# A hand-written statement order ahead of the main loop, replaced on four engines

## The chip, the cores and the metric

One core of one Trainium2 chip runs the whole program. The metric is device microseconds of that core, the median of three runs.

## What is computed

A block of 2048 tokens of width 512 goes through three layers, each with a residual: half a router layer, an attention layer, half a router layer. Cut to what matters here:

```python
def ffn(h):                         # router layer, on layernorm(x)
    logits = h @ router_weight.T + router_bias        # 64 experts
    w = top8(softmax(logits))
    return h * w.sum() + w_dense @ expert_bias
x = x + 0.5 * ffn(layernorm(x))
x = x + attention(layernorm(x))     # 8 groups of 4 heads, chunks of 128 tokens,
                                    # decay from cumulated g = softplus(x @ Win.T + dt_bias) * A
x = x + 0.5 * ffn(layernorm(x))
```

## The kernel before, in words

The tokens are 4 blocks (f = 0 to 3) of 4 chunks (i = 0 to 3) of 128. The attention runs as a long loop of 8 groups times 16 steps, one chunk a step, and its code in `step` is the same in both kernels. Ahead of the first step, every engine has its own straight list of calls; that list is written out by hand, one for TensorE (from line 999), ScalarE (from 1251), GpSimd (from 1498) and VectorE (from 1747). Engines wait for each other only through semaphores, and each engine works strictly down its list. What these lists do for each block:

- `pe_turn` (L530) transposes a chunk of x, `act_turned` (L540) copies it out as FXT, `pe_logits` (L557) multiplies it with the router weights. `dve_stats(dve, 0, ...)` (L463, L468) and `pool_rstd` (L478 to L483) make the layernorm's scale.
- `dve_logits` (L568 to L576), `dve_choose` (L582, L585), `act_exp` (L611) and `dve_weigh` (L592 to L604) pick eight experts. `pe_weights` (L621) and `act_weights` (L626) transpose the weights as FWT; `pe_mix` (L649, L650) multiplies them with the expert biases. The mix of block 0 also waits for `lows_ready`, which GpSimd raises after two operations, FEBL and WINL (L1508).
- `pool_scales` and `pool_residual` (L674) scale x, `dve_mixed` (L705) adds the mix.
- `dve_stats(dve, 1, ...)`, `act_normalise` (L715, tile XN), `pe_turn2` (L724), `act_turned2` (L730, XTH) and `dve_turned2` (L737, XTL) make the attention's input.
- `pe_dt` (L349 to L351 on WINH, WINL), `dve_dt_in`, `dve_dt_abs`, `dve_series` (L783 to L805, on 256 columns: blocks 0 and 1 as q = 0, blocks 2 and 3 as q = 1) make g. The last operation of `dve_series(dve, 0, 3)` writes NG (L805). `pe_sums`, `act_sums`, `pe_rows`, `act_rows` turn it, the SP queue sends it to memory and reads it back broadcast (ROWS), and GpSimd masks it (`mask_rows`, L1462).
- `fill(0, 0, k)` for k = 0 to 9 are the first block's projections: K, four Q, V, four gates. `swap`, `times_sin`, `times_cos`, `add_sin` rotate K and Q; `gate` (L1194) and `silu2` (L1661) finish the gates; `decay` (L1207), `decayed` (L1676), `p_hi` (L1213) and `p_lo` (L1484) build the attention weights of a chunk, `weighted_v` (L1472) and `wv_lo` (L1480) the weighted values.

The first projection inside step 0, called fill A below, goes into a bank that `silu2(0, 0, 3, 9)` must have read; `bank_free` has that wait. `decay(0, 1)` on ScalarE waits for `p_lo(0, 0)`, since both use the tile PF.

Of the kernel before, what the change touches and what calls it, by code (L numbers as in the profile page):

```python
# [19 lines left out]
ALU = mybir.AluOpType  # L20
ACT = mybir.ActivationFunctionType
# [15 lines left out]
FAR = 1.0e30  # L37
# [87 lines left out]
def build(nc, x, cos, sin, masks, wall, rwt, rb, eb2, wint, dtb, alog, gn, out):  # L125
    rows_dram = nc.dram_tensor("rows_dram", (NCH, KVH, GW), F32).ap()
    with ExitStack() as ctx:
# [46 lines left out]
        AFTER = sb("AFTER", [P, P])  # L174
# [669 lines left out]
        def _(pe):  # L844
# [158 lines left out]
            pe_turn(pe, 0, (0, 1))  # L1003
# [17 lines left out]
            pe_weights(pe, 1)  # L1021
            pe_turn2(pe, 0, (0,))
            pe_mix(pe, 1, (0, 1))
            pe_turn2(pe, 0, (1,))
            pe_mix(pe, 1, (2,))
            pe_turn2(pe, 0, (2,))
            pe_mix(pe, 1, (3,))
            pe_turn2(pe, 0, (3,))
            pe_logits(pe, 2, (2, 1, 0))
            pe_turn(pe, 3, (0,))  # L1030
            pe_logits(pe, 2, (3,))
            pe_turn(pe, 3, (1,))
# [114 lines left out]
        def _(act):  # L1147
# [833 lines left out]
```

## Time and profile before

| what | value |
|---|---|
| median of 3 runs | 1702.77 us (1702.34 to 1702.81) |
| profiled execution, its time | 1706.06 us |
| its span | 1704.2 us |
| mean granted TensorE clock | 0.989 |
| TensorE matmul busy | 97% of the span |
| VectorE, GpSimd, ScalarE busy | 83%, 72%, 66% |

The profiled execution took 3.3 us more than the median of the runs; 1.9 us of its time lies outside the span. Busy shares are means over the whole program: the stretch that the change touches is the first 105 us.

### The profile page before, as it was taken

Reading aid. Unit: us, or ns where it says so; the run is one execution under the profiler, and the core shown is the slowest. Engines: PE = TensorE matmul, PEld = TensorE weight load, DVE = VectorE, ACT = ScalarE, POOL = GpSimd, SP = SyncE. Lnnn points to the kernel's source line nnn. Section 1 sums busy time; section 2 is a strip of 40 time slices with the busy share of each in tenths; the row PEclk is TensorE's granted clock in tenths of the full one; section 3 lists DMA queues with packets and bytes.
Section 4 is the critical chain, followed back from the end, with each engine's and each line's share of the span. In section 5 each row is a group of like instructions: output and inputs, shape, how many; then the busy total and the mean of one; then the engine's idle time right before and its main releaser. Section 6 shows DMA issues by size and latency. Waiting matters only on the chain.

```text
span 1704.2 us, 34810 instructions
## 1 busy us (share of the span) xinstructions
PE 1650.2 (97%) x11470; PEld 954.6 (56%) x11668; DVE 1410.6 (83%) x3089; ACT 1119.9 (66%) x3019; POOL 1231.9 (72%) x1204
## 2 busy tenths in 40 slices
PE   7898999999999999999999999999999999999987
PEld 5554555555555555555555555555555555555554
DVE  6988788787878888787888888788888888788887
ACT  4775676766666667666766667666766666666653
POOL 4676677777777777776868768676777777777755
PEclk8999999999999999999999999999999999999998
DMA  5111011010111012010111011110110102110002
GB/s 209 32 35 52 21 45 63 32 39 20 57 50 51 20 32 75 19 51 26 57 51 44 20 38 57 38 50 20 44 63 32 38 20 64 45 37 20 26 13 100
DMA packets 39059, 76.91 MB, mean 45 GB/s; under 512 B 4832, under 2 KB 5856, under 8 KB 37856
## 3 DMA queue, kind: packets, MB, share of 16 engines
q1 hardware_dynamic: 38880, 74.66, 13.8%
q8 instruction: 95, 1.56, 0.4%
q14 instruction: 84, 0.69, 0.1%
HBM read 70.19 MB, written 4.46 MB: 44 GB/s over the span
## 4 chain that ended last, share of the span: by engine, by line
PE 76%; POOL 8%; DVE 7%; issue 5%; ACT 3%; DMA 1%; SPq 0%; DVEq 0%; POOLq 0%; ACTq 0%
PE B L350 24%; PE B L351 23%; PE B L349 22%; PE B L962 3%; POOL QS L1449 1%; PE B L557 1%; POOL WVF L1472 1%; POOL ROWS L1462 1%; POOL PL L1484 1%; PE B L909 1%; POOL RR L1491 1%; POOL WL L1442 1%; ACT QS L1170 1%; POOL KL L1456 1%; DVE ST L1706 1%
## 5 line engine op out<-in xcount | busy, mean ns | idle before, releaser
L1484 POOL TENSOR_TENSOR PL<-PF,PH 128x512 bf16<-128x512 f32 x128 | 158.2, 1236 | 300.0 <-ACT PH L1213 300.0
L351 PE MATMUL B<-WH,XTL 128*128 128x128 bf16 (+1 forms) x992 | 269.3, 296 | 1.6
L1213 ACT ACTIVATE PH<-PF 128x512 bf16<-128x512 f32 x128 | 80.7, 630 | 278.7 <-DVE PF L1676 278.7
L350 PE MATMUL B<-WL,XTH 128*128 128x128 bf16 (+1 forms) x961 | 257.6, 294 | 1.7
L349 PE MATMUL B<-WH,XTH 128*128 128x128 bf16 (+1 forms) x960 | 257.2, 294 | 0.6 <-DVE QF L1641 0.6
L350 PE MATMUL B<-XTL,WH 128*128 128x512 bf16 x640 | 243.3, 380 | 1.7
L1449 POOL TENSOR_TENSOR QS<-QS,SIN 128x512 f32<-128x512 f32 x160 | 204.6, 1279 | 47.0 <-ACT QS L1170 47.0
L349 PE MATMUL B<-XTH,WH 128*128 128x512 bf16 x609 | 231.5, 380 | 3.2 <-DVE G L1661 1.0
L351 PE MATMUL B<-XTH,WL 128*128 128x512 bf16 x610 | 231.8, 380 | 0.0
L1725 DVE SCALAR_TENSOR_TENSOR YF<-B,RR,G 128x128 f32<-128x128 f32 x512 | 143.9, 343 | 72.4 <-POOL RR L1491 72.4
L1207 ACT ACTIVATE PF<-ROWS,NG 128x128 f32<-128x128 f32 x512 | 162.8, 391 | 47.1 <-POOL ROWS L1462 46.8
L350 PE MATMUL B<-WL,ZTH 128*128 128x512 bf16 x480 | 181.9, 379 | 0.1
L351 PE MATMUL B<-WH,ZTL 128*128 128x512 bf16 x479 | 181.5, 379 | 0.0
L349 PE MATMUL B<-WH,ZTH 128*128 128x512 bf16 x478 | 181.2, 379 | 0.1
L1676 DVE SCALAR_TENSOR_TENSOR PF<-B,DT,PF 128x128 f32<-128x128 f32 x512 | 143.3, 340 | 42.9 <-PE B L351 39.3
L1685 DVE TENSOR_TENSOR YF<-B,EG 128x512 f32<-128x512 f32 x120 | 82.7, 689 | 103.8 <-PE B L962 103.8
L1462 POOL TENSOR_TENSOR ROWS<-ROWS,AFTER 128x512 f32<-128x512 f32 x128 | 162.7, 1272 | 2.7 <-DMA ROWS<-rows_dram 2.7
L1491 POOL TENSOR_TENSOR RR<-RM,HALF 128x4 f32<-128x4 f32 x128 | 144.3, 1128 | 10.1 <-POOL RM L1488 0.2
L1236 ACT ACTIVATE YF<-B 128x128 f32<-128x128 f32 x512 | 133.6, 275 | 11.8 <-DVE B L1692 10.7
L1480 POOL TENSOR_TENSOR WVL<-WVF,WVH 128x512 bf16<-128x512 f32 x120 | 139.0, 1159 | 0.0
L1472 POOL TENSOR_TENSOR WVF<-VF,WJ 128x512 f32<-128x512 f32 x120 | 138.3, 1152 | 0.1
L1646 DVE TENSOR_TENSOR QF<-QF,QS 128x512 f32<-128x512 f32 x128 | 131.3, 1027 | 6.9 <-POOL QS L1449 5.4
(213 smaller groups left out, 4474.2 us busy)
## 6 DMA issues: line engine op xcount, KB each, us to landing
ROWS<-rows_dram SPq DMA_DIRECT2D x128, 256.0 KB, 3.3
STAGE<-in_wall SPq DMA_DIRECT2D x108, 256.0 KB, 2.8
ACC<-in_x SPq DMA_DIRECT2D x3, 1024.0 KB, 9.9
out<-ACC SPq DMA_DIRECT2D x3, 1024.0 KB, 3.9
ACC<-in_x SPq DMA_DIRECT2D x4, 256.0 KB, 3.9
COS<-in_cos SPq DMA_DIRECT2D x1, 1024.0 KB, 12.2
SIN<-in_sin SPq DMA_DIRECT2D x1, 1024.0 KB, 14.5
out<-ACC SPq DMA_DIRECT2D x4, 256.0 KB, 4.3
```

The source lines that it names most:

```text
L349: nc.tensor.matmul(out_, ah, bh, start=first, stop=False)
L350: nc.tensor.matmul(out_, ah, bl, start=False, stop=False)
L351: return nc.tensor.matmul(out_, al, bh, start=False, stop=last)
L1207: ins = nc.scalar.activation(PF[:, c], ROWS[:, n % 2, c], ACT.Exp, bias=tab(NG, g, n)[:, h:h + 1], scale=-1.0)
L1449: nc.gpsimd.tensor_tensor(QS[:, sl, :], QS[:, sl, :], SIN[:, t0:t0 + TB], ALU.mult).then_inc(sin_ready.sem, 1)
L1462: nc.gpsimd.tensor_tensor(rows, rows, AFTER[:, None, :].broadcast_to([P, G, P]), ALU.add).then_inc(rows_masked.sem, 1)
L1472: nc.gpsimd.tensor_tensor(WVF[:, :, :], VF[b % 2][:, None, s * P:(s + 1) * P].broadcast_to([P, G, P]), tab(WJ, g, n)[:, :, None].broadcast ...
L1480: nc.gpsimd.tensor_tensor(WVL[:, :], WVF[:, :, :].rearrange("p h e -> p (h e)"), WVH[:, :], ALU.subtract).then_inc(wvl_ready.sem, 1)
L1484: nc.gpsimd.tensor_tensor(PL[:, n % 2, :], PF[:, :], PH[:, n % 2, :], ALU.subtract).then_inc(pl_ready.sem, 1)
L1491: nc.gpsimd.tensor_tensor(RR[:, :], RM[:, :], HALF[:, :], ALU.pow).then_inc(rr_ready.sem, 1)
L1676: ins = nc.vector.scalar_tensor_tensor(PF[:, c], B_S[:, c], dt[:, h:h + 1], PF[:, c], ALU.mult, ALU.mult)
L1725: ins = nc.vector.scalar_tensor_tensor(YF[:, c], B_PV[:, c], RR[:, h:h + 1], G2[:, s + b % 2 * (s == BLK - 1), c], ALU.mult, ALU.mult)
```

## The change

Only the four lists ahead of the first step change. The same calls are made with the same arguments, apart from how the chunks of a block are grouped into calls; the function bodies, `step`, the SP queue's list and the buffers stay. The core of the diff, TensorE first, then ScalarE, GpSimd and VectorE:

```diff
             pe_turn(pe, 0, (0,))
             pe.wait_ge(ones_ready.sem, 1)
             pe_centre(pe)
-            pe_turn(pe, 0, (2,))
+            pe_turn(pe, 0, (1,))
             pe_logits(pe, 0, (0,))
-            pe_turn(pe, 0, (3,))
+            pe_turn(pe, 0, (2, 3))
             pe_logits(pe, 0, (1, 2, 3))
-            pe_turn(pe, 1, (0, 1))
+            pe_turn(pe, 1, (0, 1, 2))
             pe_weights(pe, 0)
-            pe_turn(pe, 1, (2,))
             pe_mix(pe, 0, (0, 1))
-            pe_logits(pe, 1, (2, 1))
-            pe_mix(pe, 0, (2, 3))
+            pe_logits(pe, 1, (0, 2, 1))
             pe_turn(pe, 1, (3,))
-            pe_logits(pe, 1, (0,))
+            pe_mix(pe, 0, (2,))
             pe_turn(pe, 2, (0,))
             pe_logits(pe, 1, (3,))
+            pe_mix(pe, 0, (3,))
             pe_turn(pe, 2, (1, 2, 3))
             pe_weights(pe, 1)
+            pe_logits(pe, 2, (0, 1))
+            pe_mix(pe, 1, (0,))
...
-            fill(0, 0, 8, None, True, 0)
             pe.wait_ge(d_in.sem, d_in.at(NB - 1, 0))
             scores(0, 0)
+            fill(0, 0, 8, None, True, 0)
+            pe_rows(pe, 1)
             fill(0, 0, 9, None, True, 0)
-            pe_rows(pe, 1)
...
+            keys_hi(0, 0)
+            gate(0, 0, 1, 7)
+            decay(0, 0)
             act_dt_exp(act, 1)
+            p_hi(0, 0)
             gate(0, 0, 2, 8)
-            decay(0, 0)
-            act_sums(act, 1)
-            keys_hi(0, 0)
-            p_hi(0, 0)
+            decay(0, 1)
             gate(0, 0, 3, 9)
             wv_hi(0, 0)
-            decay(0, 1)
             act_rows(act, 1)
...
             pool_scales(pool, 0)
+            pool_residual(pool, 0, (0,))
             nc.gpsimd.tensor_tensor(WINL[:, :, :], WINF[:, :, :], WINH[:, :, :], ALU.subtract).then_inc(lows_ready.sem, 1)
-            pool_residual(pool, 0)
+            pool_residual(pool, 0, (1, 2))
...
             pool_wj(pool, 0)
-            lo(0, 0, 0)
+            pool_wj(pool, 1)
             lo(0, 0, 3)
             lo(0, 0, 4)
             mask_rows(0, 0)
             mask_rows(0, 1)
-            pool_wj(pool, 1)
...
-            dve_turned2(dve, 3, (1, 2, 3))
             silu2(0, 0, 1, 7)
-            dve_dt_in(dve, 3)
-            q_lo(0, 0, 1)
-            dve_dt_abs(dve, 1)
-            q_lo(0, 0, 2)
+            decayed(0, 0)
             dve_series(dve, 1, 0)
-            decayed(0, 0)
-            nc.vector.tensor_scalar(GNH[:, :], GN[:, :], 0.5, None, ALU.mult).then_inc(const_dve.sem, 1)
-            keys_lo(0, 0)
             silu2(0, 0, 2, 8)
             silu2(0, 0, 3, 9)
```

**TensorE, blocks 0 and 1.** L530 is a transpose, L557 logits (4 rows a chunk), L621 the weights' transpose, L649 and L650 one mix, L724 the second transpose. Before, from the logits of block 0:

```order
L557 MATMUL B<-RWT,FXT 128x64 x12
L530 MATMUL B<-IDF,ACC 128x128 x8
L621 MATMUL B<-IDB,FWHL 128x128 x4
L530 MATMUL B<-IDF,ACC 128x128 x4
L649 MATMUL B<-FEBH,FWT 128x512
L650 MATMUL B<-FEBL,FWT 128x512
L649 MATMUL B<-FEBH,FWT 128x512
L650 MATMUL B<-FEBL,FWT 128x512
L557 MATMUL B<-RWT,FXT 128x64 x8
```

The same place with the change:

```order
L557 MATMUL B<-RWT,FXT 128x64 x12
L530 MATMUL B<-IDF,ACC 128x128 x12
L621 MATMUL B<-IDB,FWHL 128x128 x4
L649 MATMUL B<-FEBH,FWT 128x512
L650 MATMUL B<-FEBL,FWT 128x512
L649 MATMUL B<-FEBH,FWT 128x512
L650 MATMUL B<-FEBL,FWT 128x512
L557 MATMUL B<-RWT,FXT 128x64 x12
L530 MATMUL B<-IDF,ACC 128x128 x4
```

The third transpose of block 1 moved ahead of the weights, and three chunks' logits instead of two now stand ahead of the other two mixes.

**VectorE, around the logits of block 1** (L568). Before:

```order
L705 SCALAR_TENSOR_TENSOR ACC<-B,FHRC,ACC 128x512 x2
L463 BN_STATS BS<-ACC 128x6 x3
L705 SCALAR_TENSOR_TENSOR ACC<-B,FHRC,ACC 128x512 x2
L463 BN_STATS BS<-ACC 128x6 x2
L468 BN_AGGR MV<-BS 128x2 x4
L568 SCALAR_TENSOR_TENSOR FLG<-B,RSTD,RB 128x64 x4
L573 MAX FMX<-FLG 128x8 x4
L576 TENSOR_SCALAR FNM<-FMX 128x4
L582 MATCH_REPLACE FW<-FMX,FLG 128x64 x4
```

With the change:

```order
L705 SCALAR_TENSOR_TENSOR ACC<-B,FHRC,ACC 128x512 x2
L463 BN_STATS BS<-ACC 128x6 x4
L568 SCALAR_TENSOR_TENSOR FLG<-B,RSTD,RB 128x64 x4
L573 MAX FMX<-FLG 128x8 x4
L576 TENSOR_SCALAR FNM<-FMX 128x4
L582 MATCH_REPLACE FW<-FMX,FLG 128x64 x4
L585 TENSOR_TENSOR FW<-FLG,FW 128x256
L705 SCALAR_TENSOR_TENSOR ACC<-B,FHRC,ACC 128x512
L592 TENSOR_TENSOR FW<-FW,FEX 128x256
```

Two of block 0's four mixed additions (L705) and two of its stats with their aggregate (L468) moved from ahead of these logits to behind them; two stats of block 2 came ahead.

**VectorE, the end of the list** (L1676 is `decayed`, L783 to L790 `dve_series(dve, 1, 0)`, L1661 `silu2`, one line less in the changed file). Before:

```order
L783 TENSOR_SCALAR WJ<-EG 128x256
L785 RECIPROCAL WJ<-WJ 128x256
L787 TENSOR_TENSOR DCH<-EG,WJ 128x256
L788 TENSOR_SCALAR DT<-DT 128x256
L790 TENSOR_TENSOR NG<-DCH 128x256
L1676 SCALAR_TENSOR_TENSOR PF<-B,DT,PF 128x128 x4
L1832 TENSOR_SCALAR GNH<-GN 128x1
L1666 TENSOR_TENSOR KDL<-B,KDH 128x512
L1661 SCALAR_TENSOR_TENSOR G<-G,B 128x512 x2
L1676 SCALAR_TENSOR_TENSOR PF<-B,DT,PF 128x128 x4
```

With the change:

```order
L1660 SCALAR_TENSOR_TENSOR G<-G,B 128x512 x2
L1675 SCALAR_TENSOR_TENSOR PF<-B,DT,PF 128x128 x4
L783 TENSOR_SCALAR WJ<-EG 128x256
L785 RECIPROCAL WJ<-WJ 128x256
L787 TENSOR_TENSOR DCH<-EG,WJ 128x256
L788 TENSOR_SCALAR DT<-DT 128x256
L790 TENSOR_TENSOR NG<-DCH 128x256
L1660 SCALAR_TENSOR_TENSOR G<-G,B 128x512 x2
L1675 SCALAR_TENSOR_TENSOR PF<-B,DT,PF 128x128 x4
```

The five operations of the series moved from ahead of the first `decayed` to between it and the last two `silu2`.

## Rows read from the trace of the kernel before

**Rows 1.** Windows: stretch, sum, PE, PEld, DVE, ACT, POOL busy, PE clock, DMA, GB/s.
```profile
20.00:30.00 10.00, 10.00 (x58) 8.49 (x56) 7.44 (x19) 2.75 (x5) 5.97 (x12) 0.67 0.61 243
60.00:70.00 10.00, 8.20 (x85) 4.47 (x85) 9.93 (x28) 5.19 (x9) 7.06 (x12) 1.00 0.01 2
133.00:134.00 1.00, 0.00 (x0) 0.00 (x0) 1.00 (x3) 0.92 (x2) 0.99 (x1) 1.00 0.67 229
400.00:800.00 400.00, 396.90 (x2734) 225.09 (x2782) 331.01 (x696) 268.25 (x722) 296.92 (x272) 1.00 0.14 41
```
**Rows 2.** Chain that ended last, in time order: start us, us, what.
```profile
89.61 1.53 DMA rows_dram<-CONST
95.55 2.67 POOL ROWS L1462 x2
137.01 1.12 PE B L909 x4
```
**Rows 3.** Timeline, PE: start us, us, operation, count [idle before, releaser].
```profile
9.40 0.61 PE L530 MATMUL B<-IDF,ACC 128*128 128x128 f32 x4
9.85 2.79 PE L557 MATMUL B<-RWT,FXT 128*128 128x64 f32 x24
...
20.56 3.52 PE L557 MATMUL B<-RWT,FXT 128*128 128x64 f32 x16
...
24.30 0.63 PE L650 MATMUL B<-FEBL,FWT 128*128 128x512 bf16 x1
24.73 0.63 PE L649 MATMUL B<-FEBH,FWT 128*128 128x512 bf16 x1
...
33.80 0.61 PE L621 MATMUL B<-IDB,FWHL 128*128 128x128 bf16 x4 [3.63 <-DVE FWHL L604]
```
**Rows 4.** Timeline, POOL, same columns.
```profile
18.29 0.43 POOL L1508 TENSOR_TENSOR WINL<-WINF,WINH 128x128 bf16<-128x128 f32 x1
18.70 3.02 POOL L674 TENSOR_SCALAR ACC<-ACC,FSCL,FBIA 128x512 f32<-128x512 f32 x4
```
**Rows 5.** Timeline, DVE, up to NG, same columns.
```profile
28.89 0.86 DVE L568 SCALAR_TENSOR_TENSOR FLG<-B,RSTD,RB 128x64 f32<-128x64 f32 x4 [0.62 <-PE B L557]
...
36.27 1.57 DVE L705 SCALAR_TENSOR_TENSOR ACC<-B,FHRC,ACC 128x512 f32<-128x512 f32 x2 [0.92 <-POOL ACC L674]
37.76 0.68 DVE L463 BATCH_NORM_STATS2 BS<-ACC 128x6 f32<-128x512 f32 x1
38.36 1.27 DVE L737 TENSOR_TENSOR XTL<-B,XTH 128x512 bf16<-128x512 f32 x2
...
52.08 0.75 DVE L705 SCALAR_TENSOR_TENSOR ACC<-B,FHRC,ACC 128x512 f32<-128x512 f32 x1 [0.61 <-PE B L650]
...
74.93 1.20 DVE L783 TENSOR_SCALAR WJ<-EG 128x256 f32<-128x256 f32 x1
...
86.64 0.42 DVE L805 SCALAR_TENSOR_TENSOR NG<-DT,ALOG 128x256 f32<-128x256 f32 x1
```
**Rows 6.** Timeline, DVE, end of the list, same columns.
```profile
94.37 0.28 DVE L783 TENSOR_SCALAR WJ<-EG 128x256 f32<-128x256 f32 x1
...
98.63 1.11 DVE L1676 SCALAR_TENSOR_TENSOR PF<-B,DT,PF 128x128 f32<-128x128 f32 x4
...
100.33 1.29 DVE L1661 SCALAR_TENSOR_TENSOR G<-G,B 128x512 f32<-128x512 f32 x2
103.15 1.12 DVE L1676 SCALAR_TENSOR_TENSOR PF<-B,DT,PF 128x128 f32<-128x128 f32 x4 [1.53 <-ACT PF L1207]
```
**Rows 7.** Timelines of POOL, ACT and PE, same stretch and columns.
```profile
98.86 0.46 POOL L842 TENSOR_TENSOR WJ<-WJ,DT 128x128 f32<-128x128 f32 x1 [0.63 <-ACT DCH L826]
...
100.49 1.16 POOL L1484 TENSOR_TENSOR PL<-PF,PH 128x512 bf16<-128x512 f32 x1
...
101.76 1.28 ACT L1207 ACTIVATE PF<-ROWS,NG 128x128 f32<-128x128 f32 x4 [0.34 <-POOL PL L1484]
...
101.67 0.54 PE L349 MATMUL B<-XTH,WH 128*128 128x512 bf16 x1 [1.05 <-DVE G L1661]
```

More of the change, by code:

```diff
@@ L1022, in _ @@
+            pe_mix(pe, 1, (1, 2))
+            pe_logits(pe, 2, (3,))
             pe_turn2(pe, 0, (0,))
[L1023 to L1026, printed above, removed]
             pe_mix(pe, 1, (3,))
[L1028 to L1032, printed above, removed]
+            pe_turn2(pe, 0, (1, 2, 3))
+            pe_turn(pe, 3, (0, 1))
@@ L1033, in _ @@
             pe_dt(pe, 0)
+            pe_turn(pe, 3, (2,))
+            pe_weights(pe, 2)
             pe.wait_ge(f_xtl.sem, f_xtl.at(0, BLK - 1))
             fill(0, 0, 0, None, True, 0)
-            pe_turn(pe, 3, (2, 3))
-            pe_weights(pe, 2)
+            pe_turn(pe, 3, (3,))
+            pe_logits(pe, 3, (2, 0))
+            pe_mix(pe, 2, (0,))
+            pe_logits(pe, 3, (3,))
             pe_turn2(pe, 1, (0,))
-            pe_logits(pe, 3, (0,))
-            pe_mix(pe, 2, (0, 1))
@@ L1299, in _ @@
             swap(0, 0, 2, 2)
+            act_dt_exp(act, 0)
             swap(0, 0, 3, 3)
-            act_normalise(act, 2, (0,))
+            split_hi(0, 8)
+            act_normalise(act, 2)
             hi(0, 0, 0)
-            act_normalise(act, 2, (1,))
-            act_dt_exp(act, 0)
             swap(0, 0, 4, 4)
-            act_normalise(act, 2, (2, 3))
+            hi(0, 0, 1)
+            act_turned2(act, 2, (0, 1, 2))
             split_hi(0, 9)
-            act_turned2(act, 2)
-            hi(0, 0, 1)
             hi(0, 0, 2)
+            act_normalise(act, 3, (0,))
+            act_turned2(act, 2, (3,))
+            act_normalise(act, 3, (1,))
+            gate(0, 0, 0, 6)
+            act_normalise(act, 3, (2,))
             values(0, 0, 5)
-            gate(0, 0, 0, 6)
-            act_normalise(act, 3)
-            gate(0, 0, 1, 7)
+            act_normalise(act, 3, (3,))
             act_turned2(act, 3, (0,))
             act_sums(act, 0)
-            act_turned2(act, 3, (1,))
             act_rows(act, 0)
             hi(0, 0, 3)
-            act_turned2(act, 3, (2, 3))
+            act_turned2(act, 3, (1, 2))
+            act_sums(act, 1)
             hi(0, 0, 4)
+            act_turned2(act, 3, (3,))
+            keys_hi(0, 0)
+            gate(0, 0, 1, 7)
+            decay(0, 0)
             act_dt_exp(act, 1)
+            p_hi(0, 0)
             gate(0, 0, 2, 8)
-            decay(0, 0)
-            act_sums(act, 1)
-            keys_hi(0, 0)
-            p_hi(0, 0)
+            decay(0, 1)
             gate(0, 0, 3, 9)
             wv_hi(0, 0)
-            decay(0, 1)
             act_rows(act, 1)
@@ L1767, in _ @@
             dve_weigh(dve, 1)
-            dve_stats(dve, 0, 2, (2, 3))
-            dve_mixed(dve, 1, (0, 1))
+            dve_mixed(dve, 0, (3,))
+            dve_stats(dve, 1, 0, (2, 3))
+            dve_stats(dve, 0, 2, (3,))
+            dve_mixed(dve, 1, (0,))
             dve_stats(dve, 0, 3, (0,))
+            dve_stats(dve, 1, 1, (0,))
+            dve_mixed(dve, 1, (1,))
+            dve_stats(dve, 0, 3, (1,))
+            dve_logits(dve, 2)
             dve_turned2(dve, 0, (0, 1))
-            dve_stats(dve, 1, 1, (0, 1))
@@ L1781, in _ @@
+            dve_stats(dve, 0, 3, (2, 3))
             dve_dt_in(dve, 0)
-            dve_weigh(dve, 2)
-            dve_stats(dve, 0, 3, (1, 2, 3))
+            times_cos(0, 0, 0, 0)
+            dve.wait_ge(c_landed.sem, 16 * 6)
+            nc.vector.tensor_scalar(GNH[:, :], GN[:, :], 0.5, None, ALU.mult).then_inc(const_dve.sem, 1)
             dve_mixed(dve, 2, (0,))
+            nc.vector.tensor_scalar(AFTER[:, :], TRIF, -FAR, FAR, ALU.mult, ALU.add).then_inc(after_ready.sem, 1)
+            add_sin(0, 0, 0, 0)
@@ L1785, in _ @@
+            dve_stats(dve, 1, 2, (0,))
             dve_turned2(dve, 1, (0,))
-            dve_mixed(dve, 2, (1,))
-            dve_stats(dve, 1, 2, (0, 1))
-            times_cos(0, 0, 0, 0)
-            dve_mixed(dve, 2, (2,))
+            dve_mixed(dve, 2, (1, 2))
             dve_logits(dve, 3)
+            dve_stats(dve, 1, 2, (1,))
+            dve_choose(dve, 3)
+            dve_weigh(dve, 3)
+            dve_turned2(dve, 1, (1,))
+            times_cos(0, 0, 1, 1)
             dve_mixed(dve, 2, (3,))
+            dve_turned2(dve, 1, (2, 3))
@@ L1813, in _ @@
             dve_series(dve, 0, 1)
-            dve.wait_ge(c_landed.sem, 16 * 6)
-            nc.vector.tensor_scalar(AFTER[:, :], TRIF, -FAR, FAR, ALU.mult, ALU.add).then_inc(after_ready.sem, 1)
             dve_series(dve, 0, 2)
```

142 lines of the change are left out of this document (70 added, 72 removed).

## Prediction

> **What bounds the kernel now.** I read the windows first. In the long loop TensorE (PE) is busy 396.90 of 400 us at a granted clock of 1.00, and nothing the change touches runs there [rows 1]. In the lists ahead of the first step it is another engine: from 60 to 70 us VectorE (DVE) is busy 9.93 us of 10, PE 8.20 [rows 1]. So I read the chain that ended last, in order of time, to see where the lists hand over. The broadcast rows leave for memory at 89.61, GpSimd (POOL) masks them from 95.55, and only at 137.01 does the chain come back to PE [rows 2]; ahead of that PE stands still, with 0.00 us busy from 133 to 134 [rows 1]. Whatever the lists lose or gain up to the rows and in the first attention weights therefore moves the whole rest, one for one, and PE's own place in its list matters only where DVE or POOL wait for it. DVE writes NG, which the rows need, at 86.64 [rows 5]. The question is when DVE gets there with the new list, and what follows it.
>
> A change within 0.2%, 3.4 us here, is what I count as no difference. The profiled execution's time is 3.3 us above the median of the runs; I sum differences against its trace and add them to the median, 1702.77.
>
> **The change, part by part.** The same operations run; only waits can differ. Up to NG the set of DVE operations is also the same, apart from two small ones, so NG comes later by exactly the waits that DVE gains.
>
> *Block 0.* Both transposes of chunks 2 and 3 now stand ahead of the last three logits; one takes 9.85 - 9.40 = 0.45 us [rows 3]. Block 0's choice, and with it GpSimd's scales, come 0.4 us later. I found no gain there, since the transpose that moved behind the centring ran in time in which PE waited.
>
> *The first mix* waits for WINL. It ran at 18.29; now one residual stands ahead of it, 3.02 / 4 = 0.76 us [rows 4]. WINL ends at 18.7 + 0.4 + 0.8 = 19.9, the mix starts at about 20.05; before, it could start right behind WINL's end at 18.7.
>
> *Logits of block 1.* PE was at 1.2 GHz here: the clock is 0.67 over 20 to 30 us, although PE is busy 10.00 of 10 [rows 1]. At that level one mix is 2 x 0.43 = 0.86 us (24.30 to 24.73 is one of its two matmuls), one chunk's logits about 1.66 (x16 is two chunks, 3.52 with the end of the last one); at 2.4 GHz a chunk's logits are 2.79 / 3 = 0.93 [rows 3]. From 20.05: two mixes 1.7, three logits 5.0, which is 26.75; the clock was back by then in the trace. At 2.4 GHz: transpose 0.45, mix 0.43, transpose 0.45, logits 0.93, in all 29.0. Before, DVE started on them at 28.89 [rows 5]. So putting one mix behind them buys nothing: it is paid back by WINL. But before, DVE had by then also done two mixed additions (0.66 each, of the x2 row), two stats (0.60, 37.76 to 38.36) and an aggregate (0.36), and only two stats less of block 2 [rows 5]: it now enters this point 1.3 + 1.2 + 0.4 - 1.2 = **1.7 us** behind, plus 0.1.
>
> *Blocks 1 to 3.* From 28.89 to 74.93, where the first series starts, DVE waited before only 0.92 and 0.61 us, 1.5 in all [rows 5]. I followed the new list with the same durations, engine by engine. It waits: 1.35 us for block 1's first mix, since two logits of block 2 stand ahead of it, PE wakes at 33.8 at 1.2 GHz [rows 3] and the copy of the weights comes first; 0.35 for XTH of chunk 2 behind ScalarE's exponentials; 0.7 for the swapped K; 0.6 for block 2's third mix, now behind two second transposes; 0.2 for the last XTH of block 1; 0.95 for `pe_dt(1)`, which needs that XTL first. Together 4.15. So the series starts 1.8 + 4.15 - 1.5 = 4.4 later by this sum; adding the operations up one by one instead gives 78.5 against 74.93, 3.6. I take 3.6: the first counts short waits of the trace as work.
>
> *To NG.* AFTER (0.14) already stands earlier, the series' first operation need not be slowed, -0.7, and the last second transpose of block 2 waits 0.4 more. NG: +3.6 - 0.4 = **+3.2 us**, at 89.8. On that slowed operation: it took 1.20 us at 74.93 and 0.28 at 94.37 [rows 5, 6]. The Trainium skill's page "SBUF — State Buffer", section "Who interferes with whom", says that a VectorE instruction in a 2-port mode blocks against GpSimd for the whole instruction. By it the sum has 0 to 0.9 us here, as GpSimd happens to lie.
>
> *Behind NG.* The send and read of the rows are unchanged, so masking is 3.2 later. For: WJ(1) is now done before the masks; it waited 0.63 and took 0.46 behind them [rows 7], 1.1 us of POOL. The first `decayed` no longer stands behind the series. But PL(0), which ran at 100.49 [rows 7], then waits for PH(0): masks end at 101.4, `decayed(0,0)` 101.4 to 102.4, PH 103.0, PL(0) 103.1 to 104.2. It is +2.6, so 0.6 of the 3.2 is won back. Against: `decay(0,1)` waits for PL(0) (it did, at 101.76 [rows 7]), and gate 3, ahead of it before, now stands behind it: 104.3 + 1.2 + 0.5 = 106.0. DVE has meanwhile the series (0.28 + 1.75 + rest, 3.3 to 4.2 us as from 94.37 to 98.63 [rows 6]), then both `silu2` (1.29 for two): the last ends at about 107.2. Fill A on PE, released by it at 101.67 before [rows 7], starts at 107.3, +5.6; `decayed(0,1)`, at 103.15 before [rows 6], starts at 107.2, +4.1. Both feed the chain to 137. PE has still time ahead of 137 to cover a part of its 5.6, `decayed` has none, so I take +4.4 in all, nearer the +4.1: tail **+1.2** on top of NG.
>
> Sum: 3.2 + 1.2 = +4.4, 1702.77 + 4.4 = **1707.2 us**. Ends of the unknown: NG could be 1 us (DVE catches up wherever its waits were my miscount) to 5 us later (4.4 plus a longer wait for block 1's mix); the tail -1.2 (only WJ gained) to +2.4 (fill A's 5.6 in full). From -0.2 to +7.4.
>
> **Rivals.**
>
> 1. *The clock stays at 1.2 GHz longer.* In the trace 10.00 us of busy PE had the clock only partly back [rows 1], and the logits are many short matmuls. With more logits ahead of the mixes the level may return a stretch later, at 26.7 and again after 33.8. Then transpose, mix, transpose, logits (2.26) take twice as long, +2.2, and block 1's mix comes 1.3 later: up to 3.5, of which DVE wins back some 1.4. +4.4 + 2.1 = 1709.3. The Trainium skill's page "TensorE: Matmul & The Clock Gate", section "What's actually happening", has the clock set by how busy PE has been. By that the longer unbroken stretch of logits should bring it back no later, and this rival is void; the row at 0.67 with PE busy throughout speaks against taking it so simply. 12%.
> 2. *No loss (the other side).* DVE's waits are made good: if the three waits of 1.35, 0.95 and 0.6 are each under 0.3, NG is 2.2 earlier than in my sum, +1.0, and the tail +1.2 or less: +2, 1704.8. It decides where block 1's first mix is done by 37.2. For it: each of these waits is a small difference of two long sums. Against: the 1.7 us of deferred work is there whatever happens. 35%.
> 3. *Faster.* All waits of DVE after 28.89 vanish (-1.5), the mix of block 0 isn't held by WINL (-1.2), and the tail keeps WJ's 1.1 and the earlier `decayed`, without series and gate counting: -3.8, 1699.0. It needs fill A not to matter. 11%.
> 4. *The change doesn't do what it says* is excluded for order (the listing shows it), but it may be masked: had PE slack of 4.4 us before 137 covered the tail, only NG's 3.2 is left, 1706.0. That lies within the forecast's or rival 2's range.
>
> **How the numbers follow.** Forecast 42%, +4.4 (+3.4 to +6.5); rival 1 12%; rival 2 35%, 1702.0 to 1706.1; rival 3 11%. Faster by over 0.2% (below 1699.4): 0.10. Within: 0.36, rival 2 and the edge of rival 3. Slower: 0.54, forecast and rival 1. The range leaves out the far half of rival 3 and the far part of rival 1: 1700.3 to 1709.8. The forecast's own range is 1706.2 to 1709.3.
>
> **What would show it.** NG at 89 to 91; WINL about 19.5; mix of block 1 read by DVE with over 1 us of wait near 38; the first series near 78.5; the rows sent near 92.8; fill A near 107 with DVE as its releaser; the chain back on PE at about 141. The forecast is wrong if NG stands before 88, or fill A before 104. Clock 0.50 in most of 27 to 30 us would be rival 1.

## The result, and the profile after

The changed kernel takes **1714.57 us** (median of 4 runs, 1713.58 to 1715.21) against 1702.55 us (1701.28 to 1702.81) for the kernel before beside it: ratio 1.0065, interval 1.0054 to 1.0077, **12.0 us slower**. The forecast had the side right, 1707.2 us, and the size wrong: its range ended at 1709.8. The execution profiled took 1715.21 us, with a span of 1713.4.

First the windows of the changed kernel (stretch, its length, PE, PEld, DVE, ACT and POOL busy, granted clock, DMA share, GB/s):

```profile
10.00:20.00 10.00, 6.25 (x41) 5.26 (x40) 7.25 (x32) 5.46 (x17) 5.18 (x12) 0.68 1.01 409
20.00:30.00 10.00, 10.00 (x44) 8.77 (x43) 4.12 (x7) 1.12 (x2) 5.67 (x9) 0.50 0.65 256
30.00:40.00 10.00, 6.75 (x36) 5.64 (x36) 8.00 (x36) 5.22 (x17) 4.38 (x13) 0.67 0.11 26
40.00:50.00 10.00, 8.36 (x48) 6.49 (x47) 7.33 (x25) 5.83 (x16) 4.09 (x7) 0.78 0.00 1
400.00:800.00 400.00, 399.45 (x2783) 225.13 (x2782) 331.34 (x696) 268.75 (x728) 296.19 (x272) 1.00 0.14 41
```

The long loop is as it was (DVE 331 us in both, clock 1.00; PE's 396.90 in [rows 1] has 49 matmul records fewer than the same window has now). From 20 to 30 us PE is busy 10.00 of 10, as before, but at 0.50 all the way where it had 0.67 [rows 1], and DVE has 4.12 us to do instead of 7.44. So the time is lost ahead of the first step. The chain that ended last (start, us, what) says how late it hands over, that is, how late the chain comes back to PE (L909):

```profile
99.28 1.53 DMA rows_dram<-CONST
...
105.06 1.01 POOL ROWS L1457
...
115.15 1.39 POOL PL L1479
...
147.16 1.12 PE B L909 x4
```

The rows go out 9.7 us later than in [rows 2] (89.61), PE takes over 10.15 us later (137.01), and the profiled times differ by 9.15 (1706.06 against 1715.21). The medians differ by more because the profile of the kernel before was of a late execution. Time minus the start of the second PL (`p_lo` of the second chunk) is 1600.1 us here, and between 1599.0 and 1601.5 in all the other profiles of this study: the whole difference is made ahead of that product.

DVE's timeline in the changed kernel (start, us, operation, count, idle time before and what ended it), to be read against [rows 5]:

```profile
30.75 0.86 DVE L568 SCALAR_TENSOR_TENSOR FLG<-B,RSTD,RB 128x64 f32<-128x64 f32 x4 [5.98 <-PE B L557]
...
41.69 0.75 DVE L705 SCALAR_TENSOR_TENSOR ACC<-B,FHRC,ACC 128x512 f32<-128x512 f32 x1 [2.76 <-PE B L650]
...
59.43 0.69 DVE L1640 TENSOR_TENSOR KF<-B,COS 128x512 f32<-128x512 f32 x1 [1.51 <-ACT QS L1168]
...
83.70 0.73 DVE L783 TENSOR_SCALAR WJ<-EG 128x256 f32<-128x256 f32 x1
...
94.86 0.43 DVE L805 SCALAR_TENSOR_TENSOR NG<-DT,ALOG 128x256 f32<-128x256 f32 x1
```

Block 1's logits come at 30.75 instead of 28.89, with DVE idle for 5.98 us ahead of them; its first mix comes after 2.76 us of waiting; the series starts 8.8 us late and NG is 8.2 late. Of these 8.8 us 1.9 are there at block 1's logits. From there to the series DVE is busy 46.03 of 52.95 us, where it was busy 43.89 of 46.04: 2.1 us of work that was put off, and 4.8 us more of idle time. PE in the same stretch, against [rows 3] and [rows 4]:

```profile
13.57 2.75 PE L530 MATMUL B<-IDF,ACC 128*128 128x128 f32 x12 [1.00 <-DMA ACC<-in_x]
17.52 0.61 PE L621 MATMUL B<-IDB,FWHL 128*128 128x128 bf16 x4 [1.20 <-DVE FWHL L604]
19.68 0.59 PE L649 MATMUL B<-FEBH,FWT 128*128 128x512 bf16 x1 [1.55 <-POOL WINL L1504]
...
21.33 5.22 PE L557 MATMUL B<-RWT,FXT 128*128 128x64 f32 x24
...
28.91 1.81 PE L557 MATMUL B<-RWT,FXT 128*128 128x64 f32 x8
...
34.67 1.09 PE L530 MATMUL B<-IDF,ACC 128*128 128x128 f32 x4 [2.56 <-ACT FXT L540]
...
37.02 3.67 PE L557 MATMUL B<-RWT,FXT 128*128 128x64 f32 x16 [0.69 <-ACT FWT L626]
```

Three chunks' logits, x24, take 5.22 us at 21.33, where the same x24 took 2.79 at 2.4 GHz [rows 3]. Windows of half a microsecond give the stretches in which the granted clock was 0.50, which is 1.2 GHz (ends to about 0.1 us). Ahead of 60 us: before 16.4 to 26.7 and 33.5 to 36.9, 13.7 us in all; changed 13.7 to 30.8, 34.2 to 44.4 and 51.2 to 54.7, 30.7 us in all.

### The profile page after: what moved, and what is told of

Its sections match the earlier page's. It is cut to its first block, busy times and chain, and to the rows that moved or that the text cites. A ratio compares the mean times of both kernels' runs of the same rounds, so it can differ in the third digit from the quotient of the medians.

```text
span 1713.4 us, 35011 instructions
## 1 busy us (share of the span) xinstructions
PE 1664.9 (97%) x11668; PEld 960.2 (56%) x11668; DVE 1410.1 (82%) x3089; ACT 1120.4 (65%) x3019; POOL 1233.5 (72%) x1204
## 3 DMA queue, kind: packets, MB, share of 16 engines
q1 hardware_dynamic: 38880, 74.66, 13.7%
## 4 chain that ended last, share of the span: by engine, by line
PE 78%; POOL 8%; DVE 6%; issue 4%; ACT 3%; DMA 0%; ACTq 0%; POOLq 0%; DVEq 0%
PE B L349 23%; PE B L351 23%; PE B L350 23%; PE B L962 3%; PE B L557 2%; POOL QS L1444 1%; POOL WVF L1467 1%; PE B L909 1%; POOL ROWS L1457 1%; POOL PL L1479 1%; POOL RR L1486 1%; POOL WL L1437 1%; PE B L530 1%; ACT QS L1168 1%; DVE YF L1724 1%
## 5 line engine op out<-in xcount | busy, mean ns | idle before, releaser
L349 PE MATMUL B<-WH,XTH 128*128 128x128 bf16 (+1 forms) x992 | 269.3, 296 | 0.0
L350 PE MATMUL B<-WL,XTH 128*128 128x128 bf16 (+1 forms) x992 | 269.3, 296 | 0.0
L349 PE MATMUL B<-XTH,WH 128*128 128x512 bf16 x640 | 242.8, 379 | 2.9 <-DVE G L1660 2.2
L351 PE MATMUL B<-XTH,WL 128*128 128x512 bf16 x640 | 242.6, 379 | 0.0
```

Of the source, the lines that this page charges most:

```text
L349: nc.tensor.matmul(out_, ah, bh, start=first, stop=False)
L350: nc.tensor.matmul(out_, ah, bl, start=False, stop=False)
L351: return nc.tensor.matmul(out_, al, bh, start=False, stop=last)
```

## Experiments

Each kernel was timed in five rounds against the kernel before on the same chip, whose median in the three batches was 1702.46, 1703.53 and 1703.65 us. Differences below are against that median. The ranges expected are absolute times. Those of the second batch (keep_after2, after_gap0, act_first, before_tail_after) were written when that median stood at 1702.46, and it was 1.1 us higher in their batch, so up to 1.1 us of a deviation there need not be the kernel's.

### The clock held in both kernels

TensorE's queue gets matmuls of zeros in its waits, into the bank that the warm-up ahead of the first transpose already uses; they add nothing to the output.

```diff
+            for i in range(6):
+                nc.tensor.matmul(B_T[:, :], WH[:, PO - 1, 0:P], WH[:, PO - 1, :], start=True, stop=True)
             pe_turn(pe, 1, (0, 1, 2))
+            for i in range(10):
...
             pe_weights(pe, 0)
+            for i in range(6):
...
             pe_mix(pe, 0, (0, 1))
...
             pe_turn(pe, 2, (1, 2, 3))
+            for i in range(14):
...
             pe_weights(pe, 1)
+            for i in range(2):
...
             pe_logits(pe, 2, (0, 1))
```

This is keep_after, the changed kernel. keep_before is the kernel before with 8, 6 and 14 of them, ahead of block 1's transposes and of the weights of blocks 0 and 1.

> The changed kernel with 38 extra matmuls of zeros into a bank that nobody reads yet, put in front of five waits of TensorE between 12 and 37 us (6, 10, 6, 14 and 2 of them), so that it stays busy there. The product is the same. Theory A (TensorE at 1.2 GHz makes the front of the new list slow: 30.7 us of the first 60 against 13.7 before): the clock stays at 2.4 GHz from 13 to 45 us, the logits of block 1 reach VectorE at 26 to 27 us instead of 30.75, block 1's first mix before 38 instead of 41.69, NG 4 to 7 us earlier, the time 1707 to 1710. Theory B (the order itself makes VectorE wait, the clock is a side effect): NG moves by less than 2 us and the time stays at 1712 or more.

> The kernel before with the same kind of zero matmuls (8, 6 and 14) in front of three waits between 12 and 33 us. Theory A: there too TensorE is at 1.2 GHz from 16.4 to 26.7 and 33.5 to 36.9; held at 2.4 the logits of block 1 come 2 to 3 us earlier, but VectorE is full from 28.9 on and waits only 4.3 us in all up to NG, so 1 to 3 us are won: 1699.5 to 1701.5. Theory B: no difference beyond 1 us, or some tenths slower where the extra matmuls stand in the way.

**keep_after**: 1710.82 us (1709.97 to 1712.44), ratio 1.0047 (1.0034 to 1.0060). **keep_before**: 1699.48 us (1698.90 to 1701.87, 11 runs), ratio 0.9982 (0.9974 to 0.9991), 3.0 us faster than the kernel before, and so than both. The clock is 1.00 from 10 to 40 us in both. Of keep_after's theory A the logits (25.93), the mix (36.98) and NG came as expected or earlier, the time 0.8 us over its range; keep_before came within 0.1 us of its range. A window of keep_before, columns as above:

```profile
20.00:30.00 10.00, 9.40 (x69) 7.05 (x68) 9.86 (x37) 4.87 (x15) 6.04 (x13) 1.00 0.55 215
```
From its DVE timeline:

```profile
31.84 1.41 DVE L705 SCALAR_TENSOR_TENSOR ACC<-B,FHRC,ACC 128x512 f32<-128x512 f32 x2 [0.27 <-PE B L650]
...
70.34 1.20 DVE L783 TENSOR_SCALAR WJ<-EG 128x256 f32<-128x256 f32 x1
```

PE is busy less (9.40 of 10) and DVE more: 9.86 us instead of 7.44. NG stands at 81.97, 4.7 us ahead of [rows 5]; in keep_after at 88.84, 6.0 ahead of the changed kernel. In keep_after the remedy itself cost a part of what it won: its 14 matmuls ran from 30.32 to 33.50 while DVE's FWHL was ready at 30.85, so they held up block 1's weights. Two more counts settle it.

keep_after2 has 6, 7, 4, 3 and 2 in the same five places. keep_after3 has 6, 7, 5, 3 and 2 there and these:

```diff
-            pe_turn(pe, 2, (1, 2, 3))
+            pe_turn(pe, 2, (1, 2))
+            for i in range(10):
...
+            pe_turn(pe, 2, (3,))
...
-            pe_turn2(pe, 0, (1, 2, 3))
-            pe_turn(pe, 3, (0, 1))
+            pe_turn2(pe, 0, (1, 2))
+            for i in range(5):
...
+            pe_turn2(pe, 0, (3,))
+            pe_turn(pe, 3, (0,))
+            for i in range(5):
...
+            pe_turn(pe, 3, (1,))
```

> The changed kernel with fewer zero matmuls in its waits: 6, 7, 4, 3 and 2 instead of 6, 10, 6, 14 and 2. In the profile of keep_after the 14 ended at 33.4 us, while VectorE's FWHL of block 1 was ready at 30.85 us, so that they held block 1's transposes of weights up by some 2.3 us, and VectorE's wait for block 1's first mix was 2.87 us. Theory (the order itself costs about what its waits on VectorE were forecast to, some 4 us at NG, the clock the rest, and the surplus matmuls hid this): clock still 1.00 in most of 10 to 40 us, the wait for block 1's first mix under 1.2 us, NG near 86.3 (keep_after 88.84, keep_before 81.97), time 1708.0 to 1709.5. Rival (the order is dear by itself, through other waits): the wait shrinks but others take its place, NG over 88, time 1710.5 or more. Second rival: with so few the clock falls again, then NG is 91 or more and the time over 1712.

> The changed kernel with zero matmuls in all waits that are over 1 us up to 45 us: also between block 2's transposes (10) and ahead of the second transposes and of block 3's (5 and 5), where keep_after2 had none and its granted clock was 0.51 to 0.64 from 42 to 46 us. Theory (keep_after2's median of 1709.9 beside its profiled 1707.1 us comes from executions in which the clock fell): median 1706.5 to 1708.5, a spread of under 2.5 us, NG near 86; against keep_before's 1699.5 us, 7 to 9 us are then the order alone (4.1 up to NG, 2.3 from there to the first gated chunk in the profiles). Rival (the order costs more in its typical execution than in the profiled one): median over 1709.

**keep_after2**: 1709.91 us (1707.10 to 1710.79), NG at 86.07 against the 86.3 expected; the time was 0.4 over its range. **keep_after3**: 1706.08 us (1704.68 to 1710.49, 11 runs), ratio 1.0016 (1.0007 to 1.0025), 0.4 under the range expected; the spread was 5.8 us and not under 2.5. Its DVE:

```profile
17.44 0.86 DVE L568 SCALAR_TENSOR_TENSOR FLG<-B,RSTD,RB 128x64 f32<-128x64 f32 x4 [7.18 <-PE B L557]
...
30.50 0.86 DVE L568 SCALAR_TENSOR_TENSOR FLG<-B,RSTD,RB 128x64 f32<-128x64 f32 x4 [1.47 <-PE B L557]
...
39.17 0.75 DVE L705 SCALAR_TENSOR_TENSOR ACC<-B,FHRC,ACC 128x512 f32<-128x512 f32 x1 [0.49 <-PE B L650]
...
54.71 0.69 DVE L1659 TENSOR_TENSOR KF<-B,COS 128x512 f32<-128x512 f32 x1 [0.45 <-ACT QS L1187]
...
78.98 0.73 DVE L783 TENSOR_SCALAR WJ<-EG 128x256 f32<-128x256 f32 x1
...
90.59 0.43 DVE L805 SCALAR_TENSOR_TENSOR NG<-DT,ALOG 128x256 f32<-128x256 f32 x1
```

The profiled execution was one of two late ones (1710.40 us): block 0's logits reached DVE at 17.44, where they come at 12.37 in keep_front, which has the same list there. Its PE shows why:

```profile
12.18 5.22 PE L557 MATMUL B<-RWT,FXT 128*128 128x64 f32 x24
17.62 2.34 PE L1011 MATMUL B<-WH 128*128 128x512 bf16 x5 [0.22 <-issue]
...
25.38 2.79 PE L557 MATMUL B<-RWT,FXT 128*128 128x64 f32 x24
```

The same x24 takes 5.22 us at 12.18 and 2.79 at 25.38, and the zero matmuls at 17.62 take 0.43 us each, which is 512 columns at 1.2 GHz. TensorE had not yet left that level, though the granted clock reads 1.00 there. It reads 1.00 as well in every other profile while the first zero matmuls take the same 0.43 us; that the record holds only changes of the level, and none had come yet, is the likely reading, not a shown one. In keep_front the full rate was reached at about 6.5 us (its x24 at 9.54 takes 2.79), here at about 20. Behind that the matmuls run at the full rate up to 66 us. The granted clock is 1.00 from there to 82 us.

Block 0's and block 1's logits are both 5.1 us later than in keep_front. That this lateness is carried on in full is an estimate. Less these 5.1 us the series starts at 73.9, NG is at 85.5 and L909 at 137.2; in keep_before they are at 70.34, 81.97 and 132.18. **With the clock held, the order costs +3.6 at the series, +3.5 at NG and +5.0 at the hand-over.** keep_after2, whose profile needs no such correction but has 3.4 us at 0.50 from 42.0 on, has +4.6, +4.1 and +6.4 (74.90, 86.07, 138.61). Held means up to about 80 us: keep_after3 is at 0.50 again from 82.5 to 85.9 and from 99.5 to 103.0, keep_before from 97.2 to 100.6, and what that costs at the hand-over was not separated.

By the medians, each against the kernel before on its chip, the order costs +2.4 against -3.0: 5.4 us, less than the 7 to 9 expected. Of the 12.0 us of the change that leaves 6.6 for the clock: the changed order loses 9.6 us by it, the old one 3.0. Each of these medians has an interval of 1.5 to 2 us either way, so 5.4 and 6.6 are good to some 2 to 3 us. Which statements of the new order make the 5.4 us was not taken apart.

### Which stretch at 1.2 GHz costs

Two kernels have keep_after's loops in a part of the places: after_gap0 only the 6 ahead of block 1's transposes, keep_front 6, 7 and 5 in the first three and none later.

> The changed kernel with six zero matmuls in one wait only, that of the transposes of block 1 for their rows of x (12.57 to 13.57 us in its profile, where the granted clock fell right after it). Theory A (that one idle microsecond makes the clock fall early, and the first three transposes then run at 1.2 GHz): the clock stays 1.00 to 16.5 us or later as in the kernel before, 1 to 2 us are won up to block 1's logits, and NG comes 1 to 3 us earlier than 94.86; time 1711.5 to 1713.5. Theory B (the clock falls wherever TensorE has idle time in 12 to 20 us, and the wait for FWHL and WINL will do as well): the clock is 0.50 from 17 us all the same and comes back no earlier than 29 us; NG within 1 us of 94.86 and time 1713.5 to 1715.5. The theory that the clock does not matter: no difference in any view.

> The changed kernel with zero matmuls in the waits of 12 to 20 us alone (6, 7 and 5), none later. Theory (the first stretch at 1.2 GHz, 13.7 to 30.6 us, makes most of the clock's part; the second, in block 1's mixes, 2 to 3 us): block 1's logits at 25.5 to 26, clock 0.50 again from about 30 to 40 us, NG 88 to 90.5 (86.07 with all waits filled, 94.86 with none), time 1710.5 to 1712. Rival (the second stretch is the dear one): NG over 91.

**after_gap0**: 1714.32 us (1712.62 to 1715.22). The trace went by theory A: the clock held to 18.3 us, was low for 20.5 us ahead of 60 instead of 30.7, and NG came at 92.75. The median stands within theory B's range as written, and within theory A's less the 1.1 us of its batch; the profiled execution was the fastest of the five. So filling this one wait buys hardly anything. Nor is it shown that the wait sets when the clock falls: after_tail (below) has no zero matmuls and the changed kernel's list up to here, and its profile kept the clock as long, to 18.6 us, although this wait was longer (1.34 us, ahead of 14.31; 1.00 in the changed kernel, where the clock fell at 13.7). In act_first it fell at 15.8. In all five profiles that have this list without zero matmuls block 1's logits come at 30.13 to 30.79, wherever the clock fell between 13.3 and 18.6: the first mix waits for WINL anyway. What makes them late is that the level is low while the logits run, from 20 us on (25.42 in keep_front, where it is not).

**keep_front**: 1712.07 us (1709.40 to 1712.49), at the end of the range expected, with NG and the clock as expected. Its profile is of the fastest execution. Its DVE:

```profile
25.42 0.86 DVE L568 SCALAR_TENSOR_TENSOR FLG<-B,RSTD,RB 128x64 f32<-128x64 f32 x4 [1.47 <-PE B L557]
...
36.35 0.75 DVE L705 SCALAR_TENSOR_TENSOR ACC<-B,FHRC,ACC 128x512 f32<-128x512 f32 x1 [2.76 <-PE B L650]
...
89.58 0.42 DVE L805 SCALAR_TENSOR_TENSOR NG<-DT,ALOG 128x256 f32<-128x256 f32 x1
```

The logits of block 1 are 5.3 us earlier than in the changed kernel, as early as in keep_before (25.14). But the clock falls from 30.4 to 40.6 us, and the wait for block 1's mix is again 2.76 us; where it was held (keep_after2, keep_after3) this wait was 0.50 and 0.49. Between profiles the first stretch is worth 5.3 us at NG, the second 3.5 (89.58 to 86.07). The medians don't give the same split: 3.6 us for the first (12.0 to 8.4), 6.0 for all later ones (8.4 to keep_after3's 2.4). Which stretch is the dear one stays open.

### One statement moved back

```diff
 mix_first, PE:
-            pe_logits(pe, 2, (0, 1))
             pe_mix(pe, 1, (0,))
+            pe_logits(pe, 2, (0, 1))
 act_first, ACT:
+            act_turned(act, 2, (0,))
             act_exp(act, 1)
             nc.scalar.activation(ALOG[:, :], ALOG[:, :], ACT.Exp).then_inc(a_ready.sem, 1)
-            act_turned(act, 2, (0, 1))
+            act_turned(act, 2, (1,))
```

> The changed kernel with one pair exchanged on TensorE: block 1's first mix ahead of two logits of block 2 rather than behind them. VectorE waited 2.76 us for that mix in the changed kernel. If this wait costs what it lasts, NG comes 2 to 2.8 us earlier and so does the end. Rival: VectorE waits instead a little later, for the logits of block 2, which all come 0.9 us later at 1.2 GHz, and less than 1 us is won.

> The changed kernel with one thing moved: on ScalarE the copy of block 2's first transposed tile stands ahead of block 1's exponentials and of ALOG's, as in the kernel before (there ahead of the exponentials too). In the changed profile TensorE waits 2.56 us at 34.67 for the copies behind them (2.65 us at 29.85 with the clock held), and weights of block 1 stand behind these transposes. Theory (the weights wait for VectorE's FWHL at 35.6 us anyway, so the transposes at 1.2 GHz delay them by under 0.5 us): NG 0 to 1 us earlier than 94.86, time 1713.5 to 1714.6. Rival (this wait is what lets the clock fall at 34.2 and carries the loss on): TensorE's second stretch at 1.2 GHz begins later or ends earlier, NG 2 us or more earlier, time under 1712.5.

**mix_first**: 1715.70 us (1714.61 to 1717.12), ratio 1.0076 (1.0062 to 1.0090). Of its two expectations the rival's came, under 1 us won; none was. The first mix is read at 38.88 instead of 41.69, and the next one simply takes the wait:

```profile
44.09 0.75 DVE L705 SCALAR_TENSOR_TENSOR ACC<-B,FHRC,ACC 128x512 f32<-128x512 f32 x1 [3.30 <-PE B L650]
...
45.65 0.86 DVE L568 SCALAR_TENSOR_TENSOR FLG<-B,RSTD,RB 128x64 f32<-128x64 f32 x4 [0.21 <-PE B L557]
```

NG stands at 94.95 (94.86). **act_first**: 1713.81 us (1712.62 to 1716.11), within the theory's range; the profile, of the latest of its five executions, has NG at 96.62, not up to 1 us earlier than 94.86, and a mix wait of 2.55. Neither single statement carries the loss.

### The tail

The last part of all four lists (from dt of block 2 on) was exchanged, both ways. Its core on DVE:

```diff
 before_tail_after, DVE:
-            silu2(0, 0, 0, 6)
-            silu2(0, 0, 1, 7)
...
-            dve_series(dve, 1, 0)
-            decayed(0, 0)
...
+            silu2(0, 0, 0, 6)
+            silu2(0, 0, 1, 7)
+            decayed(0, 0)
+            dve_series(dve, 1, 0)
```

> The changed kernel with the ends of its four lists, from the second transpose of block 3 on, in the order of the kernel before. The prediction put the tail at +1.2 us (series and gate 3 ahead of the second chunk's attention weights against the earlier WJ and first decay). The traces say NG +8.2 and the second PL +10.1, so +1.9: by that the time is 1 to 2 us below the changed kernel's. Rival: the tail is even, since the two gains in it pay for the two losses, and the time stays within 0.5 us.

> The kernel before with the changed kernel's last part alone on all four engines (from dt of block 2 on: sums, rows, keys, fills 8 and 9, the lows and gates). Theory (the tail costs 1 to 2 us by itself: NG to the second product PL was 20.3 us in the changed profile against 18.4 before): NG within 0.7 of 86.64, the second PL near 106, time 1703.3 to 1704.6. Rival (the tail only costs where the front is late, since it was ordered for another front): 1702.0 to 1703.0. Third: the front's lateness made the tail's +2: then before and this differ by nothing in NG to second PL.

**before_tail_after**: 1703.66 us (1702.38 to 1705.07, 11 runs) against 1703.53, ratio 1.0000 (0.9991 to 1.0009): the new tail alone costs nothing that can be measured, to 1.5 us either way. The theory that it costs 1 to 2 us had NG near 86.64 and the second PL near 106; they stand at 83.45 and 102.50. NG to the second PL is 19.05 us in its profile, 18.37 before. **after_tail**: 1713.45 us (1709.03 to 1715.28), ratio 1.0055 (1.0041 to 1.0068), against 1.0065 for the change: 1.0 us less, with intervals of 2 us either way, so not told apart from none. The profile of before_tail_after also shows how far the old front varies:

```profile
83.45 0.42 DVE L805 SCALAR_TENSOR_TENSOR NG<-DT,ALOG 128x256 f32<-128x256 f32 x1
```

This is the front of the kernel before, 3.2 us earlier than in [rows 5]. Here the clock was low from 13.2 to 20.0 and 30.3 to 33.7 us, 10.2 us in all instead of 13.7, and block 1's logits came at 25.77 instead of 28.89; the time was 1702.38 where it was 1706.06.

### The front, half and half

Both lists hold the same statements up to block 1's weights, so one can be continued with the other there.

```diff
 first_before: the old order up to these, the new one behind; first_after: the other way round
 PE   up to pe_weights(pe, 1)      ACT  up to act_weights(act, 1)
 DVE  up to dve_weigh(dve, 1)      POOL up to block 1's pool_residual
```

> The order of the kernel before on all four engines up to block 1's weights (pe_weights(1), dve_weigh(1), act_weights(1), block 1's residuals on GpSimd), and the changed order from there on. Theory (the loss begins in the first two blocks: with their order TensorE idles in 12 to 20 us and then has the logits of block 1 in one row at 1.2 GHz): block 1's logits reach VectorE as in the kernel before (27 to 29 us), NG at 86.5 to 90 (that is, only the order's own cost of 2 to 4 us in blocks 2 and 3 is left, of 83.45 and 86.64 in two profiles of the old front), time 1705.5 to 1708.5. Rival (the first half is harmless, blocks 2 and 3 and the tail make the loss): NG 92 or more, time 1711 or more. Rival 2 (the blocks' later order is free and all the loss is in the first half): NG under 86.5, time 1702.5 to 1704.5.

> The other half: the changed order up to block 1's weights, and the order of the kernel before from there on. Theory: block 1's logits reach VectorE at 29 to 31 us as in the changed kernel, and NG comes 4 to 7 us later than in the kernel before (88 to 92), time 1707 to 1710; with first_before's loss this adds up to the 12 us of the whole change. Rival (the halves don't add up, the clock's second fall belongs to the meeting of both): each half alone costs under 3 us.

**first_before**: 1712.29 us (1708.96 to 1712.78), +8.6, ratio 1.0049 (1.0037 to 1.0062). **first_after**: 1710.93 us (1707.78 to 1713.93), +7.3, ratio 1.0045 (1.0032 to 1.0057). Expected were +2 to +5 and +4 to +7 (times to 1708.5 and 1710): both cost more. Block 1's logits came at 25.16 in first_before, earlier than the 27 to 29 expected; in first_after NG came at 93.01, later than 88 to 92. The profile of first_before, of the fastest of its five executions, has NG at 89.82, which is within the theory's range; its median is within the rival's. Together they make 15.9, more than the 12.0 of the whole: the halves don't add up, though with intervals of 2 us on each the 3.9 between them are only just clear of noise. In first_before the first half runs even faster than in [rows 5], and then:

```profile
35.99 0.75 DVE L705 SCALAR_TENSOR_TENSOR ACC<-B,FHRC,ACC 128x512 f32<-128x512 f32 x1 [4.40 <-PE B L650]
```

Its clock is low from 29.0 to 39.2 us, again in the logits of block 2 that stand ahead of and between block 1's mixes. In first_after it is low from 13.3 to 30.3 and 33.8 to 44.0, and DVE waits 5.98 and 3.99 us. Each half of the new order has a stretch at 1.2 GHz of 10 us or more in which DVE then waits for a mix, and either half loses more than half of the 12.0 us. That these stretches make the loss is argued from the waits here; neither half was run with the clock held.

All kernels in one view; the stretches at 0.50 are those that begin ahead of 60 us:

| kernel | median, us | against before | us at 0.50 | NG in its profile |
|---|---|---|---|---|
| before | 1702.55 | | 13.7 | 86.64 |
| changed | 1714.57 | +12.0 | 30.7 | 94.86 |
| keep_before | 1699.48 | -3.0 | 0 | 81.97 |
| keep_after3 | 1706.08 | +2.4 | 0, but see its PE rows | 90.59 (5.1 late from the start) |
| keep_after2 | 1709.91 | +6.4 | 3.4 | 86.07 |
| keep_after | 1710.82 | +8.4 | 3.4 | 88.84 |
| keep_front | 1712.07 | +8.4 | 10.2 | 89.58 |
| after_gap0 | 1714.32 | +10.8 | 20.5 | 92.75 |
| act_first | 1713.81 | +10.3 | 27.3 | 96.62 |
| mix_first | 1715.70 | +13.2 | 30.7 | 94.95 |
| after_tail | 1713.45 | +11.0 | 23.9 | 96.10 |
| before_tail_after | 1703.66 | +0.1 | 10.2 | 83.45 |
| first_before | 1712.29 | +8.6 | 17.1 | 89.82 |
| first_after | 1710.93 | +7.3 | 27.3 | 93.01 |

The time at 0.50 is no measure of the loss by itself: after_tail and act_first have less of it than the changed kernel and NG later. keep_after2's profile is of the fastest of its six executions; its other times (1707.8 to 1710.8) say that this list, too, ran slower as a rule than the profile shows. Why was not looked into, and its 6.4 us is no measure of the order.

## Why the prediction was right in its direction and wrong in its size

- **What bounds the kernel: right.** DVE up to NG, then the chain; nothing in the loop.
- **Block 0, +0.4: not seen.** Its logits reach DVE at 12.61, in the kernel before at 12.68.
- **The first mix held by WINL: right.** WINL ended at 19.11 + 0.43 = 19.54, the mix started at 19.68 with WINL as its releaser (forecast 19.9 and 20.05).
- **Logits of block 1 at 29.0: this step failed**, in the clause "the clock was back by then in the trace". Up to there the sum held: three logits ended at 26.35 (forecast 26.75). The last transpose, mix, transpose and logits then ran at 1.2 GHz and took about 4.2 us, not 2.26, so 30.5 for 29.0. The moment at which the clock had come back in one execution of the old list was taken over to a new list. That was rival 1, given 12% and +2.1 us beyond the forecast. Its stated sign, 0.50 in most of 27 to 30 us, is what the trace shows; its price was too small. It put 2.2 us on the first stretch and 1.3 on block 1's mix and let DVE win back 1.4, 2.1 in all; by the medians the clock made 6.6 us. In the forecast itself this term stood at nothing.
- **Blocks 1 to 3, waits of 4.15 us in all, series +3.6: with the clock held the sum was met** (+3.6 in keep_after3 against keep_before, +4.6 in keep_after2), but not its parts, so in part by luck. From block 1's logits to the series keep_after3's DVE has 2.1 us more work than keep_before's (45.82 against 43.76; forecast 1.7) and 1.2 us more idle time, where the waits were summed up to 2.65 more (4.15 - 1.5). Block 1's first mix waited 0.49 where 1.35 was forecast, and 1.47 came ahead of block 1's logits. With the clock as it went, the wait for the mix was 2.76 and the series +8.8.
- **NG +3.2: right with the clock held (+3.5, or +4.1 by keep_after2), wrong as it ran (+8.2).**
- **Slowed first operation of the series:** 0.73 us instead of 1.20, so -0.5 where -0.7 was forecast.
- **Tail +1.2: the profile has more, the times can't tell.** Second PL 20.3 us behind NG against 18.4, `decayed(0,1)` 18.4 against 16.5 (+1.9, forecast +0.9), fill A at 113.42 with DVE as its releaser, +3.5 beyond NG's lateness (forecast +2.4). "The send and read of the rows are unchanged" failed by 1.4 us: they went 4.4 us behind NG, 3.0 before, since PE had a second transpose of block 3 (96.44) ahead of the sums (96.91), and NG had been ready at 95.29. By the times the new tail behind the old front costs 0.1 us, with an interval (0.9991 to 1.0009) that holds 1.2 as well as none.
- **The rivals.** No loss and faster fell: block 1's mix had to be read by 37.2 and was read at 41.69. The sum of order alone, +4.4, is near the 5.4 of the medians and the 5.0 of the traces, closer than the misses in its parts deserve; the +12 is this and a clock term that was set to nothing.

The Trainium skill's page "TensorE: Matmul & The Clock Gate", section "What's actually happening", has the clock set by how busy PE has been; by that, as the prediction said, PE busy for longer brings the clock back no later and rival 1 is void. The prediction kept the rival at 12% against it, on the row at 0.67. The trace contradicts this use of the page: PE is busy 10.00 of 10 us from 20 to 30 at 0.50, and the clock comes back at 30.8.

## What to carry to other kernels

When an order is changed where TensorE has waits, its clock is a term of the sum: work out what the same list costs at 1.2 and at 2.4 GHz and keep both, since the moment of return in one trace belongs to that list and that execution. A list that leaves the follower (here DVE) without other work in that stretch is hit harder: DVE had 4.12 us to do from 20 to 30 us instead of 7.44, and the changed order lost 9.6 us to the clock where the old one lost 3.0. Cheap matmuls of zeros in the waits tell the order's own cost from the clock's, and here they also made the best kernel; but each has to end before its wait does, as the 14 in keep_after show, which ended at 33.50 where the wait would have ended at 30.85.

## What the runs showed of the hardware

- Busy time alone did not bring the clock back. Low stretches of 17 us (13.7 to 30.8 changed, 13.3 to 30.3 in first_after) held through ten microseconds with TensorE busy in each; in first_before it was low for only 15.3 to 18.7. What decides was not found.
- When the clock falls varies between executions of one list: TensorE's list is the same in the changed kernel, mix_first, act_first, after_tail and first_after up to block 1's weights, and the fall came at 13.7, 13.9, 15.8, 18.6 and 13.3 us. The idle time ahead of block 1's transposes does not order them (1.00, 2.02, 2.86, 1.34 and 1.72 us).
- The times of the kernel before lie in two groups (1701.5 to 1702.6 and 1703.7 to 1705.1 us in the last batch). Its front has two profiles, and they go with the clock: 10.2 us at 1.2 GHz ahead of 60 us at 1702.38, 13.7 at 1706.06. Two profiles are few for this; it stays likely, not shown.
- The kernel begins at 1.2 GHz, and when it leaves that level varies: between 4.8 and 7.3 us in thirteen profiles, at about 20 in keep_after3's, with TensorE busy for 3.9 to 5.0 of the 5.0 us from 2.5 on in all fourteen, and for 4.9 in keep_after3's. Against keep_front that cost 5.1 us, and the granted clock read 1.00 throughout; the durations of equal matmuls showed it, not the clock's column. One other of its eleven executions was as late (1710.49 us). The zero matmuls did not prevent it: the eight of the start and the first six of the experiment lie in that time.
- A transfer moves the front as well: TensorE's wait for block 1's rows of x ended at 13.57 us in the changed kernel's profile, at 14.90 in keep_after's and at 15.38 in act_first's.
